# Attention and experts on one core: low parts of the weights from SBUF, a ring of twelve, and one order of work per engine

## The reference

```
out = x + attention(xn) + experts(xn)
attention: 16 heads of 32 columns, q, k, v = xn W + b
           scores = q k^T / sqrt(32) + slope_h * (key position - last position), causal
           softmax over the keys, times v; all heads together times Wo, + bo
experts:   8 experts of 256 hidden columns, the best 2 by softmax(router(rmsnorm(xn) * norm_w)),
           silu(gate) * up, down, weighted, times 4
```

## Time and profile before

| | |
|---|---|
| median of 3 runs | 1972.61 us (1968.24 to 1977.61) |
| profiled execution, span from first to last instruction | 1970.9 us |
| instructions | 39142 |
| busy share of the span | PE 96%, PEld 72%, DVE 76%, ACT 71%, POOL 70% |
| stage of the 32 heads | about 336 to 1485 us |

### The profile page before, as it was taken

One profiled execution on the slowest core, in us unless ns is written; L12 is line 12 of the kernel. 1 busy time (PEld: TensorE's weight loads), 2 busy tenths in 40 slices (PEclk: granted clock), 3 DMA queues, 4 the chain that ended last, 5 costly groups with the idle time before them and its releaser, 6 DMA issues. The chain is left out here.

```text
span 1970.9 us, 39142 instructions
## 1 busy us (share of the span) xinstructions
PE 1897.6 (96%) x8656; PEld 1425.0 (72%) x8657; DVE 1501.2 (76%) x3466; ACT 1400.8 (71%) x2728; POOL 1372.3 (70%) x1183
## 2 busy tenths in 40 slices
PE   6999999999999999999999999999998989999997
PEld 5787777676767777777677776776756767887876
DVE  6454566888989989899899898898966965666654
ACT  4333322998999989999999899998973335555554
POOL 4111113898988989889889898898948846666664
PEclk9999999999999999999999999999999999999998
DMA  8577758242242432423324224243226766656554
GB/s 268 193 260 258 272 179 283 75 114 64 73 104 61 97 80 63 113 62 81 96 62 108 69 71 106 61 96 81 62 72 183 252 197 118 104 103 104 104 99 66
DMA packets 119241, 242.13 MB, mean 123 GB/s; under 512 B 17632, under 2 KB 54368, under 8 KB 112896
## 3 DMA queue, kind: packets, MB, share of 16 engines
q1 hardware_dynamic: 101120, 205.84, 36.0%
q0 software_dynamic: 18080, 35.81, 10.3%
HBM read 139.28 MB, written 104.21 MB: 124 GB/s over the span
## 5 line engine op out<-in xcount | busy, mean ns | idle before, releaser
L1173 POOL TENSOR_TENSOR probs_lo<-probs,probs_hi 128x512 fp32r<-128x512 f32 x781 | 984.1, 1291 | 158.6 <-ACT probs L1208 156.7
L1207 ACT ACTIVATE probs_hi<-s_ps 128x512 fp32r<-128x512 f32 x905 | 602.0, 665 | 84.3 <-DVE s_ps L1280 80.2
L1208 ACT ACTIVATE probs<-s_ps 128x512 f32<-128x512 f32 x964 | 613.3, 670 | 9.8 <-DVE s_ps L1280 6.4
L1259 DVE TENSOR_REDUCE m_part<-m_ps 128x1 f32<-128x512 f32 x744 | 491.1, 685 | 9.5 <-PE m_ps L1500 5.9
L1516 PE MATMUL s_ps<-q_st,k_st 100*128 100x512 f32 (+3 forms) x880 | 327.9, 413 | 16.5 <-ACT probs L1208 11.8
L1500 PE MATMUL m_ps<-k_st,q_st 98*128 98x512 f32 (+2 forms) x840 | 282.0, 377 | 0.3 <-DVE m_part L1256 0.3
L1535 PE MATMUL o_ps<-probs_hi,v_split 128*96 128x512 f32 (+3 forms) x720 | 266.8, 380 | 1.7 <-POOL probs_lo L1173 1.7
L1536 PE MATMUL o_ps<-probs_lo,v_split 128*96 128x512 f32 (+3 forms) x720 | 259.2, 363 | 0.0
L1256 DVE CUSTOM_DVE_ANT_0 m_ps<-m_ps,mask_row 128x128 f32<-128x128 f32 x496 | 242.0, 498 | 22.5 <-PE m_ps L1500 16.3
L1516 PEld LDWEIGHTS s_ps<-q_st,k_st 100*128 100x128 f32 x880 | 161.5, 190 | 103.0 <-ACT probs L1208 37.9
L621 POOL TENSOR_TENSOR v_rows<-v_raw,v_rows 128x512 fp32r<-128x512 f32 x32 | 41.2, 1291 | 229.4 <-ACT v_rows L677 229.4
(11 more groups left out here) (236 smaller groups left out, 3658.2 us busy)
## 6 DMA issues: line engine op xcount, KB each, us to landing
v_d<-v_rows SPq DMA_DIRECT2D x7, 3072.0 KB, 9.4
v_split<-v_d SPq DMA_DIRECT2D x22, 768.0 KB, 8.5
k_st<-k_hi_d SPq DMA_DIRECT2D x44, 256.0 KB
q_st<-q_hi_d SPq DMA_DIRECT2D x44, 256.0 KB
xn_d<-xs SPq DMA_DIRECT2D x8, 1024.0 KB, 11.7
q_hi_d<-qk_hi SPq DMA_DIRECT2D x32, 256.0 KB, 8.0
q_lo_d<-qk_lo SPq DMA_DIRECT2D x32, 256.0 KB, 7.9
k_hi_d<-qk_hi SPq DMA_DIRECT2D x32, 256.0 KB, 3.5
```

The costliest lines, as they stand in the source:

```text
L1173: nc.gpsimd.tensor_tensor(*low_operands(u), ALU.subtract).then_inc(lo_ready_pool, 1)
L1207: nc.scalar.activation(probs_hi[:, P_SLOT[u]], scores, ACT.Exp, scale=SCALE)
L1208: nc.scalar.activation(scores if kind == "Q" else probs[:, P_SLOT[u]], scores, ACT.Exp, scale=SCALE).then_inc(p_ready, 1)
L1259: V.tensor_reduce(top, scores, AX.X, ALU.max).then_inc(m_taken, 1)
```

## The change

The kinds of the units change: Q is gone, D takes its place. For a D unit ACT writes `probs_hi` and `probs` into the ring as for P, and DVE instead of POOL makes the low part, with both inputs from SBUF. Before there were 25 P, 4 Q, 5 W in a head; now there are 26 P, 5 D (units 1, 5, 16, 23, 28), 3 W (8, 18, 33). PE frees a score bank for reuse when ACT is done, for all kinds.

`probs_lo` now lies on the same memory as `probs`: the low part overwrites the full weights. With two buffers instead of three the ring has 12 slots.

```diff
-KIND = "PPWPPPPPPWPPPPQPPPWPPQPQPPWPPWQPPP"
+KIND = "PDPPPDPPWPPPPPPPDPWPPPPDPPPPDPPPPW"
-ORDER = ("SMMMVVVMVMMVLSSMVMLLSMVMMVOVSLMSMVSLSMLMLVSMSMVSLMLMLVMMOVSMSSVMMSVMVMDOSLMVLLSVSMVSVMSMVSMMVSMVMSLD"
-         "LVSLMLLVMDLSMVSMMSSVMSVLSVXWVSLVLLDSOVSVLLS")
-BACK = {'V': 8, 'L': 4, 'O': 1}
+ORDERS = {"PE": ("MMMSVMSMMSVVSMVSMVMSVMSVSVMSVMSMSVVMMSMSVMSMVMSVMVMSMMVMSVSMSMVMSSVVMMSMSMVMSVMSVMSVVMMSMSVSMMVMSVSV"
+              "WSVVSVVSV"),
+          "ACT": ("OSSSSSSSSSOSSSSOSSSSSSOSSSSSSSSSSSSSSS"),
+          "DVE": ("MMSMSMMMSDMMMOMSDSMMMOMMMMMMMMMOMSMSMMSMMMMDMMMOMMMMMMMXDWSDS"),
+          "POOL": ("LLLLLLLLLLLLLLLLLLLLLLLLLL"),}
+BACK = {("PE", "V"): 9, ("ACT", "O"): 2, ("DVE", "O"): 2, ("POOL", "L"): 5}
-P_RING = 9
+P_RING = 12
-P_SLOT = [*range(8), *range(9), *range(8), *range(9)]
+P_SLOT = [0, 1, 2, 3, 4, 5, 6, 7, 8, 9, 10, 11, 0, 1, 2, 3, 4, 5, 6, 7, 8, 9, 10, 11, 0, 1, 2, 3, 4, 5, 6, 7, 8, 9]
...
+    due = [*range(3 - len(waiting["O"]), 3)] + [u + LAST_LAG + 3 for u in LAST_UNIT]
-    order, late = [], BACK["V"]
+    order = waiting["D"]
...
+        probs_at = nc.sbuf_base
         probs = sb(ctx, "probs", [P, P_RING, CH], F32)
+        probs_lo = nc.alloc_sbuf_tensor_at("probs_lo", [P, P_RING, CH], F32R, offset=probs_at)
         probs_hi = sb(ctx, "probs_hi", [P, P_RING, CH], F32R)
-        probs_lo = sb(ctx, "probs_lo", [P, P_RING, CH], F32R)
...
-                for kind, u, back in ATTEND if maxima else LAST_ATTEND:
+                for kind, u, back in (ATTEND if maxima else LAST_ATTEND)["DVE"]:      # SyncE
                     if kind == "O" and (before or not back):
                         store_context(n - back, u)
...
-                nc.scalar.activation(scores if kind == "Q" else probs[:, P_SLOT[u]], scores, ACT.Exp,
+                nc.scalar.activation(probs[:, P_SLOT[u]], scores, ACT.Exp,
                                      scale=SCALE).then_inc(p_ready, 1)
...
             def low_part(n, u):
                 dve.wait_ge(p_ready, NS * n + u + 1)
-                V.tensor_tensor(probs_lo[:, P_SLOT[u]], s_ps[:, S_BANK[u]], probs_hi[:, P_SLOT[u]].bitcast(F32),
-                                ALU.subtract).then_inc(lo_ready_dve, 1)
+                V.tensor_tensor(*low_operands(u), ALU.subtract).then_inc(lo_ready_dve, 1)
...
                 if not (first and back):
-                    if kinds(n - back)[held] == "Q":
-                        pe.wait_ge(lo_ready_dve, low_count(n - back, held))
-                    else:
-                        pe.wait_ge(p_ready, NS * (n - back) + held + 1)
+                    pe.wait_ge(p_ready, NS * (n - back) + held + 1)
```

More of the change, by code:

```diff
@@ L136, with attend_order @@
 S_BANK = [u % S_BUFS for u in range(NS - 1)] + [1]
[L139 to L143, removed]
+def attend_order(engine):
+    units = {"S": [u for u in range(NS) if engine != "DVE" or s_diagonals(u)], "M": list(range(NM)), "V": list(range(NS)),
+             "X": [0], "W": [0], "L": [u for u in range(NS) if KIND[u] == "P"],
+             "D": [u for u in range(NS) if KIND[u] == "D"], "O": list(range(S // CH))}
     order, seen = [], collections.Counter()
-    for kind in ORDER:
-        at = seen[kind] - BACK.get(kind, 0)
+    for kind in ORDERS[engine]:
+        at = seen[kind] - BACK.get((engine, kind), 0)
         order.append((kind, units[kind][at], int(at < 0)))
         seen[kind] += 1
-    assert all(seen[kind] == len(units[kind]) for kind in units)
+    assert all(seen[kind] == len(units[kind]) for kind in seen)
     return order
-ATTEND = attend_order()
+ATTEND = {engine: attend_order(engine) for engine in ORDERS}
 LAST_KIND = "".join("PW"[u in LAST_WHOLE] for u in range(NS))
@@ L159, in last_order @@
 def last_order():
[L161 to L164, removed]
+    waiting = {k: sorted({(k, u, 1) for order in ATTEND.values() for kind, u, back in order if kind == k and back})
+               for k in "VLDO"}
+    due = [*range(3 - len(waiting["O"]), 3)] + [u + LAST_LAG + 3 for u in LAST_UNIT]
     waiting["V"] += [("V", u, 0) for u in range(NS)]
@@ L167, in last_order @@
     waiting["O"] += [("O", u, 0) for u in range(S // CH)]
-    due = [2] + [u + LAST_LAG + 3 for u in LAST_UNIT]
-    order, late = [], BACK["V"]
+    order = waiting["D"]
     for u in range(NS + LAST_LAG + 4):
@@ L184, in last_order @@
             due.pop(0)
-    assert not any(waiting.values())
+    assert not any(waiting[kind] for kind in "VLO")
     return order
-LAST_ATTEND = last_order()
+LAST_ORDER = last_order()
+LAST_ATTEND = {engine: [token for token in LAST_ORDER if not token[2] or token in ATTEND[engine]] for engine in ORDERS}
 LOOPS = (NH - 2) // HEADS_RING
@@ L1175, in step_n @@
             def step_n(n, before=True):
-                for kind, u, back in LAST_ATTEND if is_last(n) else ATTEND:
+                for kind, u, back in (LAST_ATTEND if is_last(n) else ATTEND)["POOL"]:
                     if kind == "L" and (before or not back):
@@ L1225, in step_n @@
             def step_n(n, before=True):
-                for kind, u, back in LAST_ATTEND if is_last(n) else ATTEND:
+                for kind, u, back in (LAST_ATTEND if is_last(n) else ATTEND)["ACT"]:
                     if kind == "S":
@@ L1447, in step_n @@
                 pieces = None if maxima else place_tokens()
-                for kind, u, back in ATTEND if maxima else LAST_ATTEND:
+                for kind, u, back in (ATTEND if maxima else LAST_ATTEND)["DVE"]:
                     if back and not before:
@@ L1524, in value_products @@
                 else:
-                    pe.wait_ge(lo_ready_dve if kinds(n)[u] == "Q" else lo_ready_pool, low_count(n, u))
+                    pe.wait_ge(lo_ready_dve if kinds(n)[u] == "D" else lo_ready_pool, low_count(n, u))
                 for qc, kt, q0, w, at in S_UNITS[u]:
@@ L1566, in step_n @@
                     pe.wait_ge(st_loaded[r1], 16 * ST_DMAS * st_round)
-                for kind, u, back in ATTEND if maxima else LAST_ATTEND:
+                for kind, u, back in (ATTEND if maxima else LAST_ATTEND)["PE"]:
                     if not maxima and (kind, u) == ("S", 9):
```

## The result

| | before | changed |
|---|---|---|
| median of 4 runs each, same chip | 1970.89 us | 2239.23 us (2232.60 to 2242.09) |
| ratio, 95% interval | | 1.1351 (1.1323 to 1.1379) |
| span of the profiled execution | 1970.9 us | 2240.2 us |
| store of O1, counted from the first product behind the gate, median of heads 8 to 23 | 21.1 us | 29.7 us |
| head, (last - first `m_rows` cast) / 30 | 35.7 us | 44.5 us |

The change makes the kernel 268 us slower. The sign is that of the forecast, and so is the gate with its queue; the forecast was 2150, range 2050 to 2205, and the time lies above it.

A forecast was written before the change was run, and what follows sets the result against it. Each head was taken to wait at a gate for maxima queued behind SyncE's loads; block 1's store 6.7 us later less 0.84 spare gives 5.9 a head, times 30 is 177, plus 2 is 179, on 1970.9: 2150 us, range 2050 to 2205.

The forecast's parts named there:

- The gate and the queue: At each head's start PE waits for maxima queued behind SyncE's loads; opens 0.54 us after the burst, 5.9 us later.
- The 13% rival: In SyncE's queue the small maxima transfers overtake the late loads; +0.4 us a head, 1985 us, chance 13%.
- the faster case: Rival: PE is the only bound and does 0.8 us less work a head; 1948 us, chance 11%.
- no change: Rival: the orders only reshuffle waits and DVE passes block 1's store early; 1973 us, chance 6%.
- The shift of O1: The context store of column block 1, with loads behind it, comes 6.7 us later against the head's start.
- M26 to M32 with masks: On DVE these maximum tiles and masks now come before block 1's store: 4.7 us.
- one more addition: On DVE, two sums instead of one carried over from the head before, ahead of block 1's store: 0.7 us.
- sooner start: DVE's first maximum in a head starts some 0.5 us sooner, as M0 now comes ahead of S0.
- Two more low parts and the lock: On DVE before block 1's store: three low parts instead of one, 1.3 us, plus 0.5 us waiting for POOL.
- the slow clock: PE's clock may fall after idling at the gate; taken as 0, with 1 us kept for the upper end.
- the 0.84 us to spare: Slack at the gate before the change, between its opening and the next head's first product; subtracted from the 6.7 us delay.
- The lock: DVE low parts with two SBUF inputs wait for POOL's subtraction, 0 to 1.29 us each; 0.5 us taken, 1.7 at full price.

The follow-up runs named there:

- b_late: The kernel before, with SyncE issuing the loads when DVE has taken maximum tile M32 instead of behind the store of column block 1; 2131.6 us.
- a_whole: The changed kernel with its five D units turned into whole weights (W), so no low part on DVE, loads left late; 2214.1 us.
- a_fill_whole: The changed kernel, loads late, with the five D units as whole weights and six unused PE matmuls on constants ahead of each gate; 2149.7 us.
- a_rows: The changed kernel with the loads of v and the two expert weights issued behind the rows of maxima instead of ahead; 2182.8 us.
- the four kernels above: Late-load kernels, with or without DVE low parts and PE filler: changed 2239.2, a_whole 2214.1, a_fill 2230.6, a_fill_whole 2149.7 us.
- a_early: The changed kernel with the loads issued when DVE has taken maximum tile M25, ahead of the store of column block 1; 2149.7 us.
- a_early_d23: a_early with the low part of unit 23 moved on DVE from before the rows of maxima to behind them; 2064.8 us.
- a_psum: The changed kernel, loads left late, with D units reading PSUM again and three low parts moved forward on DVE; 2238.0 us.
- a_early_psum: The changed kernel with loads issued at M25, D units reading PSUM again and three low parts moved forward on DVE; 2136.2 us.
- b_sbuf: The kernel before, with the full weights of the four Q units written to the ring, so DVE subtracts from SBUF instead of PSUM; 2134.6 us.
- a_fill: The changed kernel with six PE matmuls on constants, results unused, ahead of each head's gate; 2230.6 us.
- a_early_mix: The changed kernel with loads issued at M25 and units 16 and 23 as whole weights, low parts of 1, 5 and 28 left on DVE; 2074.1 us.

## Why the prediction was wrong in size

**The gate and the queue: right.** The maxima land with the burst; the gate opens 0.6 us behind the last load (0.54 forecast). From the first load to the landing of the maxima it takes 13.0 us in the changed kernel, 13.2 in b_late, 13.0 in a_whole and 13.1 in a_fill_whole, wherever the loads start. What the gate costs is therefore, in these late kernels, when the first load goes out. b_late and a_rows show it from both sides. Not tried were maxima sent by another engine's queue, so whether they wait for their place in SyncE's queue or for busy DMA engines stays open. The 13% rival, maxima that pass the burst, is dead, and so are the faster case (PE's 0.8 us bought nothing) and no change.

**The shift of O1: the step that failed.** Forecast 6.7 us a head, measured 8.8 in the head read (8.6 at the median). Term by term: M26 to M32 with masks 4.7, measured 4.6; one more addition 0.7, measured 0.6; sooner start -0.5, measured -0.45. Two more low parts and the lock 1.3 + 0.5, measured 3.0. DVE's idle time in front of O1, for which the sum has no term as the slow clock was put at 0: +1.0. That is where the time lies. What held O1 is told by the four kernels above: the term that failed is the slow clock's. With the clock kept up the shift is 27.9 - 21.1 = 6.8, the forecast's 6.7, and the restart adds 1.7. That 6.8 comes so close is partly luck: there too the low parts cost 3.0 instead of 1.8, while DVE starts 0.9 us sooner instead of 0.5 and is idle 0.4 us less than before (means of heads 8 to 23).

**The rest of the 89 us between 2150 and 2239.** They are 3.0 us a head: 2.1 for the shift of O1 (8.8 - 6.7); 0.4 as the burst is longer (13.9 against 13.5 us at the median from the store of O1 to the last landing); and 0.5 because the 0.84 us to spare was that of one head. At the median of heads 8 to 23 the kernel before opens its gate 0.84 us behind the last load, and less 0.54 that leaves 0.3. A slip of the working besides: the lower end is 6.2 - 0.84 - 0.9 = 4.5, not 4.3.

**The lock: right that it exists, its bound wrong.** I bounded its price by one subtraction of POOL's, 1.29 us, from the earlier trace rows. In front of O1 that holds (0.5 and 1.1 us), though I took a third of it. Behind the fold unit 23 waited 4 us: the bound itself is wrong, because DVE can lose to POOL again and again. That did not set the gate in the changed kernel, where the burst is later still. It stopped PE for 2.3 us in 24 of the heads, one of the pauses after which the clock was down. With early loads it does set the gate: a_early to a_early_d23 is 85 us. The Trainium skill, page "SBUF — State Buffer", section "Who interferes with whom", says that a DVE instruction with two SBUF inputs contends with a GpSimd one that reads SBUF; the runs agree: in all seven with such low parts beside POOL's the longest last 3.4 to 4.7 us, while with the first input in PSUM (before, a_psum, a_early_psum) all take 0.7. For the 2-port modes it adds that who issues first has the ports for the whole instruction; read as a wait of at most one instruction, which is how I priced it, it falls short of 4.7 us measured for 0.67 us of work.

**The slow clock: forecast 0, at most 1 us; it is 1.7 to 2.7.** Window of the changed kernel behind a gate, columns of the earlier trace rows: granted clock 0.50, that is 1.2 GHz, after PE's stops of 2.3 and 2.6 us.

```profile
870.05:875.20 5.15, 5.14 (x15) 4.11 (x16) 3.44 (x12) 2.17 (x4) 1.28 (x1) 0.50 0.00 0
875.20:880.00 4.80, 4.80 (x24) 3.76 (x23) 3.96 (x12) 4.42 (x9) 3.47 (x3) 0.99 0.00 0
```

Filling the pause moved O1 by 1.7 us a head with the low parts in place and by 2.7 without them, where it gained 2214.1 - 2149.7 = 64 us. My argument for 0 was that DVE runs behind PE and so hides it. The trace says otherwise: without low parts DVE is idle 4.7 us in front of O1 at the slow clock and 2.7 with the filler. a_early_d23 shows the same inside one kernel: of its heads 3 to 24, nine have the half clock behind the gate and send their loads 24.0 us after PE's first product behind the landing of the maxima; the other thirteen do it at 22.7.

The forecast of 2150 equals the time of a_fill_whole, 2149.7. That is luck: it has whole units in place of the low parts, its O1 is at 27.0 and not at 27.7, and its burst is longer.

**What else was to be seen.** PE's share is 89% (88 forecast), the maxima take 3.7 us (3 or more), low parts of over 0.9 us are there. PE's idle time of 5 us once a head is two stops of 2.3 and 2.6 us, the first of which I had not foreseen, since the V carried over wait for unit 23.

## What to carry to other kernels

Where small urgent transfers share a queue with a large prefetch, the step that issues the prefetch is on the critical path; give it a place of its own instead of hanging it on a store whose place an order of work may move. Don't give VectorE a subtraction with both inputs in SBUF while GpSimd streams such work back to back: move its first input to PSUM, or place it where GpSimd is idle, and look at every instance, not the median. When taking away a suspect changes nothing, see whether another holds the same place, and whether the probe costs time of its own: a filler for PE that outlasts the pause hides what it saves, so look at the event that it is to move, not at the total alone.

## What the runs showed of the hardware

Whether DVE gets in between two subtractions of POOL depends on where in POOL's instruction it arrives. Over the low parts on DVE in seven kernels (the changed one, b_sbuf, a_early, a_fill, a_rows, a_early_d23, a_early_mix) that began while a subtraction of POOL ran and another started within 0.2 us of its end, counted by the time that the running one still had to go:

| left of POOL's subtraction when DVE's low part starts | DVE next | POOL next |
|---|---|---|
| 1.10 to 1.28 us | 215 | 0 |
| 0.98 to 1.10 us | 0 | 31 |
| 0.62 to 0.80 us | 126 | 0 |
| 0.36 to 0.53 us | 16 | 170 |

The bands take turns; none of these low parts began between them, so the table tells no period. Of the 201 that lost once none got in while another subtraction was ready: 62 waited for two more and 139 for three, until POOL had run dry. What arbitrates was not tried by itself. POOL's subtractions follow each other every 1.25 us. When DVE wins, its 0.55 us go straight into POOL's next subtraction, which then lasts about 1.7 instead of 1.29 us.
